# A residual chain of four layers: y and the centred product in the adapter's PSUM bank, and a new order on five engines

## The reference

```python
# layer 0: scores, masked softmax, pooled rows
attn_in = tanh(x @ W1 + b1); scores = attn_in @ v
p = softmax(where(mask[kind], scores, -1e30)); x = x + (p @ x) / cnt
# layer 1: an adapter chosen by language, then a layer norm
h = relu(x @ w1[lang] + b1[lang]); y = x + h @ w2[lang] + b2[lang]
x = x + (y - mean(y)) * rsqrt(var(y) + 1e-5) * gamma[lang] + beta[lang]
# layer 2: Laplacian along columns and rows (reflected) and a reaction term
x = x + zX * lap_x(x) + zY * lap_y(x) + zR * x * (1 - x)
# layer 3: a 512 x 512 product chosen by category (64 of them)
x = x + x @ W[cat] + b[cat]
```

## Time and profile before

| what | value |
|---|---|
| median of 3 runs | 1126.54 us (1125.31 to 1127.78) |
| the profiled execution | 1125.75 us |
| its span in the trace | 1124.0 us |
| TensorE busy (matmul) | 1058.5 us, 94% |
| VectorE busy | 980.7 us, 87% |
| GpSimd busy | 777.3 us, 69% |
| ScalarE busy | 498.8 us, 44% |
| DMA | 273.94 MB, mean 244 GB/s |

### The profile page before, as it was taken

How to read it: one execution, slowest core, us unless ns; L and a number is a source line. 1 busy time by engine, 2 the same in 40 slices (tenths; PEclk the granted TensorE clock), 3 DMA queues, 4 the chain that set the end, 5 groups by cost and what they waited for, 6 DMA issues and landing times.

```text
span 1124.0 us, 23427 instructions
## 1 busy us (share of the span) xinstructions
PE 1058.5 (94%) x4892; PEld 666.8 (59%) x4892; DVE 980.7 (87%) x1965; ACT 498.8 (44%) x1410; POOL 777.3 (69%) x652
## 2 busy tenths in 40 slices
PE   2589999999999999999999999999999999999997
PEld 1456566665656656666665666665666566556563
DVE  3188998998899899999999999898999899999885
ACT  0144444444444444444444444454454444444441
POOL 0066677777677677687777777668767777777776
PEclk7699999999999999999999999999999999999999
DMA  9478889887988988877777878788788788888883
GB/s 382 160 216 254 245 245 273 229 232 224 279 255 240 292 260 259 243 207 230 236 226 233 236 234 263 228 276 249 235 251 262 228 261 239 272 271 227 235 249 115
DMA packets 136181, 273.94 MB, mean 244 GB/s; under 512 B 29288, under 2 KB 29296, under 8 KB 128496
## 3 DMA queue, kind: packets, MB, share of 16 engines
q1 hardware_dynamic: 97600, 202.45, 59.5%
q10 hardware_dynamic: 38448, 70.01, 20.5%
HBM read 248.26 MB, written 33.55 MB: 251 GB/s over the span
## 4 chain that ended last, share of the span: by engine, by line
POOL 41%; issue 36%; DVE 10%; PE 9%; DMA 2%; DVEq 1%; POOLq 0%; ACT 0%; ACTq 0%; SPq 0%
POOL b_wide L817 14%; POOL rstd L790 9%; POOL neighbours L798 8%; POOL react L804 7%; DVE x L709 3%; DVE res L684 3%; PE ps_out L391 3%; POOL above L810 2%; DMA xts<-in_xT 2%; PE bank_hidden L345 2%; PE ps_attn L323 1%; PE ps_pool L364 1%; PE ps_adapt L373 1%; DVE normed L667 1%; DVE mix L659 1%
## 5 line engine op out<-in xcount | busy, mean ns | idle before, releaser
L391 PE MATMUL ps_out<-w3s,x3T 128*128 x1024 | 489.7, 601 | 2.3 <-ACT x3T L442 2.3
L810 POOL TENSOR_TENSOR above<-above,below 128x512 f32<-128x512 f32 x128 | 173.6, 1356 | 192.0 <-DMA above<-x 189.6
L391 PEld LDWEIGHTS ps_out<-w3s,x3T 128*128 128x128 f32 x1024 | 185.2, 191 | 189.9 <-issue 188.3
L790 POOL TENSOR_TENSOR rstd<-var_eps,minus_half 128x1 f32<-128x1 f32 x128 | 126.9, 991 | 137.4 <-DVE var_eps L676 137.4
L709 DVE SCALAR_TENSOR_TENSOR x<-above,zy_t,react 128x512 f32<-128x512 f32 x128 | 201.8, 1577 | 10.5 <-POOL above L810 10.4
L817 POOL TENSOR_TENSOR b_wide<-b_wide,x 128x512 f32<-128x512 f32 x128 | 179.4, 1401 | 1.8 <-DMA b_wide<-in_b 1.8
L804 POOL TENSOR_TENSOR react<-react,x 128x512 f32<-128x512 f32 x128 | 178.5, 1395 | 2.5 <-ACT react L485 2.5
L345 PE MATMUL bank_hidden<-w_all,xts 128*128 x1024 | 142.8, 284 | 24.6 <-DMA xts<-in_xT 24.6
L345 PEld LDWEIGHTS bank_hidden<-w_all,xts 128*128 128x128 f32 x1024 | 127.8, 196 | 50.0 <-issue 47.0
L463 ACT ACTIVATE square_junk<-y,neg_mean 128x512 f32<-128x512 f32 x128 | 92.4, 722 | 122.3 <-DVE neg_mean L640 122.3
L323 PE MATMUL ps_attn<-xts,w_attn 128*128 128x128 f32 x1024 | 139.0, 280 | 0.0
(11 more groups left out here) (97 smaller groups left out, 1248.3 us busy)
## 6 DMA issues: line engine op xcount, KB each, us to landing
w3s<-in_w SPq DMA_DIRECT2D x128, 1024.0 KB
xts<-in_xT ACTq DMA_DIRECT2D x128, 256.0 KB, 4.7
xs<-in_x ACTq DMA_DIRECT2D x128, 256.0 KB, 5.2
b_wide<-in_b SPq DMA_DIRECT2D x128, 256.0 KB, 4.6
out_x<-res SPq DMA_DIRECT2D x128, 256.0 KB, 3.2
below<-x SPq DMA_DIRECT2D x128, 252.0 KB
above<-x SPq DMA_DIRECT2D x128, 252.0 KB
below<-x SPq DMA_DIRECT2D x256, 2.0 KB
```

Of the source, the lines that this page charges most:

```text
L391: mm = pe.matmul(ps_out[j.ring(2)][:, :], x3T[:, j.ring(2), k * P:(k + 1) * P], w3s[:, bass.ds(wslot * (K * D) + k * D, D)], start=(k == 0 ...
L790: nc.gpsimd.tensor_tensor(rstd[:, q:q + 1], var_eps[:, q:q + 1], minus_half[:, :], ALU.pow).then_inc(rstd_ready, 1)
L810: nc.gpsimd.tensor_tensor(above[:, q, :], above[:, q, :], below[:, q, :], ALU.add).then_inc(rows_ready, 1)
```

## The change

y and normed lose their SBUF buffers: both names now mean the bank ps_adapt. `add_adapted` writes y over the product, `variance` reads it there, `center` writes the centred product over y, `normalize` reads it. Hence `center` waits for `variance`, and `adapter_up` of the next item waits for x2 in place of y. All five slot functions get a new order. `category` and `result` handle item s-5 in slot s, before s-4; `normalize` s-2, before s-1; `add_rows` stays at s-3. In the diff, steps of TensorE's and ScalarE's slots also lose the lead of one slot that they had.

```diff
-        y = sb("y", [P, 2, D])
-        normed = sb("normed", [P, D])
+        y = normed = ps_adapt
# SyncE
             def slot(s):
                 if s.inside(B):
                     cat, fresh, wslot = load_params(sp, CAT, 3, s)
+                    load_b3(s, cat)
                     shift_rows(s)
+                if (s - 3).inside(B):
+                    item_m3, = load_params(sp, ITEM, 1, s - 3)
+                    store(s - 3, item_m3)
+                if s.inside(B):
                     load_w3(s, cat, fresh, wslot)
-                if (s - 2).inside(B):
-                    item_m2, = load_params(sp, ITEM, 1, s - 2)
-                    store(s - 2, item_m2)
-                if s.inside(B):
-                    load_b3(s, cat)
# TensorE: waits
             def attn_project(a):
                 r = a.ring(2)
+                pe.wait_ge(xT_in[r], a.dma())
...
             def adapter_project(s, lang):
-                pe.wait_ge(xT_in[s.ring(2)], s.dma())
-                if s.is_at_least(2):
-                    pe.wait_ge(relu_ready, s.upto(2))
+                if s.is_at_least(1):
+                    pe.wait_ge(relu_ready, s.upto(1))
...
             def adapter_hidden(f):
-                if (f + 1).inside(B):
-                    pe.wait_ge(xw_ready, (f + 1).upto())
+                pe.wait_ge(xw_ready, f.upto())
...
                 if g.is_at_least(1):
-                    pe.wait_ge(y_ready, g.upto(1))
+                    pe.wait_ge(x2_ready, g.upto(1))
# VectorE
             def center(h, lang):
                 dve.wait_ge(mean_ready, h.upto())
+                dve.wait_ge(var_ready, h.upto())
```

More of the change, by code:

```diff
@@ L273, in slot @@
                     cat, fresh, wslot = load_params(sp, CAT, 3, s)
+                    load_b3(s, cat)
                     shift_rows(s)
+                if (s - 3).inside(B):
+                    item_m3, = load_params(sp, ITEM, 1, s - 3)
+                    store(s - 3, item_m3)
+                if s.inside(B):
                     load_w3(s, cat, fresh, wslot)
-                if (s - 2).inside(B):
-                    item_m2, = load_params(sp, ITEM, 1, s - 2)
-                    store(s - 2, item_m2)
-                if s.inside(B):
-                    load_b3(s, cat)
-            run_slots(slot, 0, B + 1)
+            run_slots(slot, 0, B + 2)
             for r in range(2):
@@ L396, in slot @@
             def slot(s):
-                h, j = s - 1, s - 4
-                if h.inside(B):
-                    pool(h)
+                h, j = s - 1, s - 5
+                if j.inside(B):
+                    wslot, = load_params(pe, WSLOT, 1, j)
                 if s.inside(B):
                     kind, = load_params(pe, KIND, 1, s)
+                    attn_project(s)
+                if h.inside(B):
+                    mix_transpose(h)
                 if j.inside(B):
-                    wslot, = load_params(pe, WSLOT, 1, j)
+                    category(j, wslot, range(0, 2))
                 if h.inside(B):
-                    lang_m1, = load_params(pe, LANG, 1, h)
+                    adapter_hidden(h)
                 if s.inside(B):
@@ L408, in slot @@
                 if j.inside(B):
-                    category(j, wslot, range(0, 1))
+                    category(j, wslot, range(2, K))
+                if h.inside(B):
+                    lang_m1, = load_params(pe, LANG, 1, h)
+                    pool(h)
+                if s.inside(B):
+                    lang, = load_params(pe, LANG, 1, s)
+                    adapter_project(s, lang)
+                if (s - 4).inside(B):
+                    x3_transpose(s - 4)
                 if h.inside(B):
                     adapter_up(h, lang_m1)
[L412 to L426, removed]
+            run_slots(slot, 0, B + 4)
         @block.scalar
@@ L462, in variance @@
                     act.wait_ge(vareps_ready, h.upto(2))
-                nc.scalar.activation(square_junk[:, :], y[:, q, :], ACT.Square, bias=neg_mean[:, q:q + 1],
+                nc.scalar.activation(square_junk[:, :], y[:, :], ACT.Square, bias=neg_mean[:, q:q + 1],
                                      accum_out=var_sum[:, q:q + 1]).then_inc(var_ready, 1)
@@ L520, in slot @@
             def slot(s):
+                if s.inside(B):
+                    item, = load_params(act, ITEM, 1, s)
+                    load_xT(s, item)
+                if (s - 2).inside(B):
+                    lang_m2, = load_params(act, LANG, 1, s - 2)
+                    relu(s - 2, lang_m2)
                 if (s - 1).inside(B):
@@ L524, in slot @@
                     reaction(s - 3)
-                if (s + 1).inside(B):
-                    item_p1, = load_params(act, ITEM, 1, s + 1)
-                    load_xT(s + 1, item_p1)
+                if (s - 5).inside(B):
+                    move_x3T(s - 5)
+                if (s - 1).inside(B):
+                    move_xw(s - 1)
+                if s.inside(B):
+                    load_x(s, item)
                 if (s - 3).inside(B):
@@ L530, in slot @@
                 if s.inside(B):
-                    item, = load_params(act, ITEM, 1, s)
-                    load_x(s, item)
+                    attn_tanh(s)
+                if (s - 1).inside(B):
+                    move_mixT(s - 1)
                 if (s - 2).inside(B):
                     variance(s - 2)
[L535 to L546, removed]
+            run_slots(slot, 0, B + 4)
         @block.vector
@@ L730, in slot @@
                     row_max(s)
-                if h.inside(B):
-                    add_b2(h, lang)
-                    add_beta(h, lang)
+                if (s - 3).inside(B):
+                    add_columns(s - 3)
+                if (s - 2).inside(B):
+                    normalize(s - 2)
                 if s.inside(B):
@@ L736, in slot @@
                 if h.inside(B):
-                    add_adapted(h)
+                    add_b2(h, lang)
                 if s.inside(B):
                     row_scale(s)
-                if h.inside(B):
-                    mean(h)
+                if (s - 5).inside(B):
+                    result(s - 5)
                 if s.inside(B):
                     mix_rows(s)
+                if h.inside(B):
+                    add_adapted(h)
+                    mean(h)
+                    add_beta(h, lang)
                 if (s - 3).inside(B):
                     add_rows(s - 3)
-                if (s - 4).inside(B):
-                    result(s - 4)
                 if h.inside(B):
@@ L820, in slot @@
             def slot(s):
[L821 to L828, removed]
                 if s.inside(B):
                     inverse_std(s)
-            run_slots(slot, 0, B + 2)
+                if (s - 2).inside(B):
+                    add_b3(s - 2)
+                if s.inside(B):
+                    sum_columns(s)
+                if (s - 1).inside(B):
+                    sum_rows(s - 1)
+                if s.inside(B):
+                    react_times_x2(s)
+            run_slots(slot, 0, B + 1)
 def kernel(x, itok_B_0_2, itok_B_0_8, condB_zX, condB_zY, condB_zR, itok_B_0_63, L0_cond_W1, L0_cond_b1, L0_cond_v,
```

4 lines of the change are left out of this document (2 added, 2 removed).

## The result

The change makes the kernel much slower: 1959.82 us, median of four runs (1953.55 to 1961.49), against 1127.16 us for the kernel before on the same chip. The ratio is 1.736, with a 95% interval of 1.729 to 1.744. The profiled execution of the changed kernel has a span of 1951.7 us. The time lies inside the range that was given, 91 us above the number, and 4 us above the band of the main forecast (1756 to 1956).

A forecast was written before the change was run, and what follows sets the result against it. TensorE bounds the kernel before; after the change a SyncE queue loop, 8.9 + 5.2 = 14.1 us an item. 84.6 + 1762.5 (125 loops) + 8.9 + 1.45 + 8.7 = 1866 us of span, forecast 1869 us, range 1700 to 2000.

The forecast's parts named there:

- the main forecast: Whole kernel: a loop of 13.2 to 14.8 us an item, so 1756 to 1956 us, given 70%; the number was 1869 us.
- The place and the mechanism: SyncE's queue: load_b3(s) waits for result(s-2) ahead of shift_rows(s), closing a loop of 14.1 us an item against 8.27.
- The sign: Changed kernel's trace: SyncE's b3 issue would start 0.2 us after result in nearly all items.
- rival B: VectorE's add_columns or normalize is held by GpSimd's b3 addition or power: +1.0, loop 15.1, 1994 us; 9%.
- From a result to the end of `sum_rows`: SyncE and GpSimd: restart 0.18, b3 issue 0.34, 0.05, six shifts 4.4, landing 2.65, sum_rows 1.27; sum 8.9 us.
- Rival D: Shifts on emptier queues: issue and landing as at the tail, loop 12.5, 1669 us; 12%.
- VectorE's part: VectorE from add_rows round to result, start to start: 5.2 us of the loop.
- the one on rstd: GpSimd: react_times_x2, then power at 0.99 us, through at 2.7 us; normalize comes at 3.0 us, so covered.
- The fill: Start of the kernel: one slot more, so the first result ends at 84.6 us instead of 76.6.
- The steps of `center` and `normalize`: VectorE: 0.60 us spacing each with PSUM, not held by GpSimd; in the trace never above 0.7 us.
- rival C: TensorE's clock stays low throughout, its work becomes 16.2 us and the bound: about 2130 us; 5%.
- Rival A: SyncE issues the shifts on x2 as before, TensorE stays the bound with a cleaner order: 1112 us; 4%.

The follow-up runs named there:

- experiment 1: The changed kernel with four b3 buffers in place of two, order kept, load_b3 waiting for the result of s-4: 1130.48 us, ratio 0.999.
- experiment 2: The kernel before with only load_b3(s) moved to the front of SyncE's slot, ahead of shift_rows(s): 1643.05 us, ratio 1.455.
- experiment 6: The changed kernel with y and normed in SBUF buffers again, all orders and waits as changed: 1968.64 us, ratio 1.739.
- experiment 5: The changed kernel with GpSimd's add_b3(s-2) moved behind sum_columns(s): 1838.3 us, ratio 1.628.
- experiment 3: The changed kernel with shift_rows(s) swapped ahead of load_b3(s) on SyncE: 1336.26 us, ratio 1.181.
- experiment 4: The changed kernel, two b3 buffers, with load_b3 of item s-1 behind shift_rows(s), and add_b3 behind sum_columns on GpSimd: 1196.07 us, ratio 1.056.

## Why the prediction was right, by its own steps

**The place and the mechanism** were right: the order of two lines on SyncE's queue. Experiments 1 and 2 show it from both sides: taking the wait away restores 1130 us, moving the one load in the old kernel makes 1643. The sign also held that named the b3 load just behind a result. But the time that came is nearer to rival B (loop 15.1, 1994 us, given 9%) than to the main forecast (1869 us, loop 13.2 to 14.8), and it lies inside the range because the range took in half of B.

**From a result to the end of `sum_rows`** 8.9 us was predicted. In the loop above it is 0.16 to the b3 load, 0.39 to the first shift, 4.48 of issue, 2.40 of landing and 1.27: 8.7. The landing of 2.65 taken from item 0 was the nearest row: over the 127 items that waited the landing has a median of 2.30 us. The tail's 1.14 and the 3.95 of full queues occur in single items (1.14 to 4.67), but not as the rule. Rival D fell. The 2.0 us of the Trainium skill (DMA: Bandwidth & Descriptors, section "Anatomy of one DMA — SWDGE (gpsimd) path") are nearer to 2.40 than the tail's row, but too little as well.

**VectorE's part** was 5.2 us and is 6.3 (1024.25 to 1030.53). This is the mis-sized term. `add_columns` took 1.62 in place of 0.74: rival B, which named the pair, at 0.88 us where it said 1.0. `add_rows` took 1.67 in place of 1.45: in the row taken the GpSimd operation beside it was `sum_columns` (1.03 us), in the new order it is `react_times_x2` (1.26 us), and the difference is the same 0.2 us. The step that failed is the one on rstd: I took the power at 0.99 us from the earlier trace rows. By the same working, power through at 2.7 us and `add_columns` at 2.3, the b3 addition would have started after `add_columns`. But those 0.99 us were themselves lengthened by `center` with two SBUF inputs; once `center` reads PSUM the power takes 0.55, and the b3 addition comes first. The relief of one step moved the collision to another. It didn't create it: with SBUF buffers (experiment 6) it is paid at `normalize`. From result 0 (start 75.22) to result 125 (1932.60) the mean loop is 14.86 us, 0.76 above the forecast, which makes 95 us in 125 loops.

**The fill** was over-counted: the first result ends at 75.9 us, not at 84.6, though it stands one slot later. The first slots, in which no category product runs yet, are short: `row_max` of items 0 to 4 starts every 5.4 to 6.5 us. That took 9 us back, which is luck: without it the time would have been 100 us above the number.

**The steps of `center` and `normalize`**: `center` takes 0.74 and not below 0.7 with its output in PSUM, and `normalize` 0.739; so the write isn't dearer than to SBUF, and reading PSUM isn't quicker. What they gain is that they are never held: `normalize` takes 736 to 743 ns in all 128 items, against up to 1759 before, and `center` 742 to 759, against up to 1109. Their spacing is 0.66 us, not the 0.60 that I counted, which is 0.1 us of the loop. The rule of the Trainium skill on the shared port (SBUF — State Buffer, section "SBUF: two separate sides") holds in all of this: experiments 5 and 6 moved a hold between steps with two SBUF inputs (`add_columns`, `mix_rows`, `normalize`), and no step with an input in PSUM took more than 0.76 us in them.

**The clock** fell in each slot, which rival C had named, but didn't stay low, which it needed. Two stretches of one loop (length, busy, with PEclk third from the end):

```profile
1000.90:1004.40 3.50, 3.50 (x11) 2.17 (x10) 1.37 (x4) 1.20 (x4) 0.00 (x0) 0.54 0.72 213
1004.80:1007.90 3.10, 3.10 (x12) 1.66 (x11) 0.00 (x0) 0.37 (x1) 0.00 (x0) 1.00 0.61 205
```

TensorE had idled 2.67 us before its work at 999.42. In the first stretch it was granted 0.54, near the lower level of 1.2 GHz, in the second 1.00; the mean of the span is 0.84. It was through with its slot before x3 came (it waited for x3 in 125 items, 2.0 us on average), so the low clock cost nothing.

**Rival A** had 4% and a time of 1112 us. With the wait gone (experiment 1) the new orders give 1130: even the gain that it assumed isn't there. That the PSUM placement in the old orders comes near to its 1112 us is a coincidence: there TensorE's wait for the mix went, and the order stayed.

**A slip** in the reading of the kernel before: VectorE's work is 0.5 us an item behind TensorE's (818.4 against 874.3 of 890 us), not 0.7, which is its distance from the period. Nothing in the sum hangs on it.

## What to carry to other kernels

When a step moves on a DMA queue, write down for every wait of that queue in which slot it is satisfied, and what stands behind it; if the consumer of what stands behind is in the same slot as the event waited for, a loop closes, and the period is the sum round it, however idle the engines are. Add up that loop before looking at busy shares. And take the duration of an operation from a row in which its neighbours are the same: a short operation that was lengthened by a neighbour will come earlier once the neighbour is relieved, and can collide with the next one. Last, look at what stands ahead of a latency-critical transfer on its queue: behind a 1 MB load the same six shifts landed 4 us later, and both repairs that kept two buffers (experiments 3 and 4) lost most of their time there.

## What the runs showed of the hardware that I had not expected

The power of one column on GpSimd takes 0.55 us, not 0.99: 0.44 us of it was a hold by VectorE's `center` with two SBUF inputs, in every one of 128 items, which is why the row looked like a plain duration (985 to 1027 ns). From the durations, a VectorE operation that waits for the port while a second GpSimd operation is due gets it between the two (experiment 2: `add_rows` takes 1.45 us beside a `sum_columns` of 1.03, and the b3 addition behind that 1.72 in place of 1.26), and a GpSimd operation that waits gets it ahead of VectorE's next (experiment 6: the b3 addition, begun during `add_columns`, takes 1.60 us, and `normalize` 1.745).

The landing of small transfers between SBUF buffers depends on what the queue holds ahead of them: a median of 5.46 us behind a 1 MB load and 1.45 us behind none, in one trace (experiment 3).
